# 16-head attention stage: the first head's probability transposes move ahead of the score matmuls in every step

## The reference, cut to what matters

```python
# self (L1_attn): 16 heads of 16 channels, causal
q, k, v = x @ Wq.T, x @ Wk.T, x @ Wv.T                  # split into 16 heads
scores = einsum('...hqd,...hkd->...hqk', q, k) / sqrt(16)
scores = where(causal, -1e9, scores)
out = einsum('...hqk,...hkd->...hqd', softmax(scores), v)
x = layernorm(x + merge_heads(out) @ Wo.T)
# cross (L1_xattn): keys and values from ctx (4, 512, 256), a mask over 512 keys, biases
q, k, v = x @ Wq.T + bq, ctx @ Wk.T + bk, ctx @ Wv.T + bv
scores = where(mask == 0, -1e9, q k / sqrt(16))
x = layernorm(x + merge_heads(softmax(scores) @ v) @ Wo.T + bo)
```

## Time and profile before

| | |
|---|---|
| median of the runs | 4162.72 us |
| the profiled execution: its time, and its span | 4165.06 us, 4163.3 us |
| busy: PE, DVE, ACT, POOL | 93%, 70%, 62%, 30% of the span |
| the 16-head stage, first to last scores | 559.05 to 1210.91 us, 652 us |
| there: PE, DVE, ACT busy | 586.6, 511.9, 455.4 us |
| one body of self attention (the second) | 74.97 us |
| one body of cross attention (the second), the last | 93.91 us, 77.45 us |

### The profile page before, as it was taken

One profiled execution on the slowest core, in us unless ns is written; L12 is line 12 of the kernel. 1 busy time (PEld: TensorE's weight loads), 2 busy tenths in 40 slices (PEclk: granted clock), 3 DMA queues, 4 the chain that ended last, 5 costly groups with the idle time before them and its releaser, 6 DMA issues.

```text
span 4163.3 us, 97842 instructions
## 1 busy us (share of the span) xinstructions
PE 3871.8 (93%) x36632; PEld 2544.0 (61%) x36632; DVE 2904.2 (70%) x10275; ACT 2580.5 (62%) x6856; POOL 1243.2 (30%) x810
## 2 busy tenths in 40 slices
PE   8979578899988999999999999999999999999996
PEld 5668445566655666666666666666666666666664
DVE  3542357788868887777777777777777777777773
ACT  2213246667766767677776676777766766767662
POOL 1103300000005433343434434333434343434330
PEclk9979789999999999999999999999999999999998
DMA  6002210000011001111011101010011101111010
GB/s 181 23 21 73 66 60 2 7 19 22 9 42 29 22 22 48 32 32 27 18 49 30 43 17 53 26 36 24 23 48 32 37 22 38 33 40 29 17 37 18
DMA packets 110785, 146.33 MB, mean 35 GB/s; under 512 B 35748, under 2 KB 77200, under 8 KB 109936
## 3 DMA queue, kind: packets, MB, share of 16 engines
q1 hardware_dynamic: 106912, 130.76, 10.9%
q0 software_dynamic: 3408, 9.31, 0.9%
HBM read 78.31 MB, written 11.40 MB: 22 GB/s over the span
## 4 chain that ended last, share of the span: by engine, by line
PE 54%; DVE 9%; POOL 4%; issue 2%; DMA 1%; ACT 0%; SPq 0%; DVEq 0%; POOLq 0%
PE psum L489 17%; PE psum L586 9%; PE psum L469 7%; PE psum L570 6%; PE psum L603 5%; PE psum L549 4%; PE psum L523 4%; POOL f_rn L892 3%; DVE f_rot L710 2%; DVE f_prob L753 1%; DVE f_rot L712 1%; DVE f_ss L717 1%; DVE f_xn L807 1%; PE psum L592 1%; DVE f_prob L781 1%
## 5 line engine op out<-in xcount | busy, mean ns | idle before, releaser
L489 PE MATMUL psum<-f_wqkv,f_xsT 128*128 128x512 f32 x2304 | 1072.1, 595 | 4.3 <-ACT f_raw L636 2.6
L887 POOL TENSOR_TENSOR f_raw<-f_rot 128x512 f32<-128x512 f32 x384 | 488.7, 1273 | 1663.8 <-DVE f_rot L712 1663.8
L650 ACT ACTIVATE f_prob<-f_prob,f_nb,f_rq 128x128 f32<-128x128 f32 x1536 | 740.1, 487 | 38.6 <-DVE f_nb L766 37.7
L489 PEld LDWEIGHTS psum<-f_wqkv,f_xsT 128*128 128x128 f32 x2304 | 402.5, 191 | 334.2 <-issue 329.4
L892 POOL TENSOR_TENSOR f_rn<-f_ss,f_half_pow 128x32 f32<-128x32 f32 x96 | 524.4, 5463 | 11.2
L586 PE MATMUL psum<-f_xnT,f_w 128*128 128x512 f32 x960 | 437.9, 595 | 2.2 <-ACT f_hT L673 1.1
L753 DVE CUSTOM_DVE_ANT_0 f_prob<-psum,f_band 128x128 f32<-128x128 f32 x1536 | 352.8, 285 | 115.9 <-PE psum L523 114.7
L634 ACT ACTIVATE f_sq<-psum 128x512 f32<-128x512 f32 x384 | 227.8, 593 | 231.1 <-PE psum L489 231.0
L781 DVE TENSOR_SCALAR f_prob<-f_prob,f_rs 128x128 f32<-128x128 f32 x1536 | 341.2, 286 | 13.6
L570 PE MATMUL psum<-f_wo,f_oT 128*128 128x256 f32 x1536 | 347.4, 379 | 1.6 <-ACT f_v L636 0.9
L710 DVE TENSOR_TENSOR f_rot<-f_raw,f_tab 128x512 f32<-128x512 f32 x384 | 333.4, 868 | 14.3 <-DMA x_before_mlp<-x_all 14.3
(11 more groups left out here) (248 smaller groups left out, 6978.3 us busy)
## 6 DMA issues: line engine op xcount, KB each, us to landing
f_v_near<-f_v SPq DMA_DIRECT2D x168, 256.0 KB, 3.5
f_wqkv<-in_Wqkv SPq DMA_DIRECT2D x36, 512.0 KB, 5.8
w_moe_W<-in_L_ffn_W SPq DMA_DIRECT2D x2, 4096.0 KB, 22.4
f_w<-in_W SPq DMA_DIRECT2D x12, 640.0 KB
f_wo<-in_Wo SPq DMA_DIRECT2D x6, 1024.0 KB, 6.4
f_xs<-x_all SPq DMA_DIRECT2D x24, 254.0 KB
expert_rows<-m_y SPq DMA_DIRECT2D x39, 128.0 KB, 1.7
h_mask_int<-in_mask_BxSxS_ik SPq DMA_DIRECT2D x16, 256.0 KB, 2.6
```

Of the source, the lines that this page charges most:

```text
L489: mm = nc.tensor.matmul(ps.ap(step), xsT[:, c, t * P:(t + 1) * P], wqkv[:, c, i * HALF:(i + 1) * HALF], start=c == 0, stop=c == KC - 1)
L650: ex = nc.scalar.activation(pr, pr, ACT.Exp, bias=nb[:, t % 2, h:h + 1], scale=rq8[:, t, h:h + 1], accum_out=sums[:, t % 2, h:h + 1])
L887: nc.gpsimd.tensor_tensor(raw[:, (4 * t + i) % 8, :], rot[:, n % 2, 0, :], rot[:, n % 2, 1, :], ALU.add).then_inc(rope_done, 1)
```

## The change

In every step the first head's transposes (`pt` 0) are written ahead of the scores (`s`), where they stood behind `s`, `max` 0 and `max` 1:

```diff
-                yield ("s", 0, n)
+                yield from [("pt", of(m), m, 0), ("s", 0, n)]
                 if n % 4 == 1:
                     t = (n - 5) // 4
                     yield ("rs", of(t), t % TB)
-                yield from [("max", 0, n, 0), ("max", 0, n, 1), ("pt", of(m), m, 0), ("e", of(e), e, 0),
+                yield from [("max", 0, n, 0), ("max", 0, n, 1), ("e", of(e), e, 0),
                             ("e", of(e), e, 1), ("pt", of(m), m, 1), *first, ("max", 0, n, 2), ("max", 0, n, 3),
                             ("pt", of(m), m, 2), ("e", of(e), e, 2), ("e", of(e), e, 3), ("pt", of(m), m, 3), *second]
```

## The result

The changed kernel takes 4170.67 us (median of 11 runs, 4165.47 to 4180.41), the kernel before 4163.18 us beside it (11 runs). The ratio is 1.0023, 95% interval 1.0016 to 1.0031: slower by about 0.2%, where 4160 and a small gain had been forecast. The time lies in the forecast range of 4150 to 4172, but on the other side of zero. Run once more beside 27 runs of the kernel before, the same code gave 1.0018 (1.0009 to 1.0027).

A forecast was written before the change was run, and what follows sets the result against it. PE was taken as fullest but not full, the engines waiting for each other in a ring. Cross bodies +0.3, last body +3.8 and self bodies -7.5 summed to -3.4 us, giving 4160, range 4150 to 4172.

The forecast's parts named there:

- the tie of `pt` 3 to the scores: Cross step 13: scores, max 0, max 1, DVE's copy of head 1, then `pt` 3 at 3.33, not shortened by the change.
- The moved head costs 0.50 between `pv` and `s`, and saves 0.465 where it stood: PE's price for head 0's transposes at 512 keys: 0.465, plus 0.03 to 0.04 for scores straight behind them.
- The bound of 0.16 extra: Scores straight behind transposes on PE: at most 0.16 extra, the tail of the last transpose, if all of it is waited for.
- the sign that I had named: The forecast would be wrong if `pv` to `s` over head 0 took much more than 1.51.
- output and empty steps: Steps with `wo` or nothing between: `pt` 3 stays at 3.33, so the step grows by 0.5.
- denominator steps: Cross steps 3, 11, 15: head 0 reaches ACT earlier, so each step gains 0.5; step 11 from 5.91 to 5.4.
- query steps: Cross steps full on PE at 5.70 before and after: change 0.
- key steps: Cross steps 2, 10, 14: the projection moves from 2.00 to 1.53, so each gains 0.3; step 10 from 6.03 to 5.73.
- The rival of the change of mode: Scores behind transposes cost more: from 0.03 more, slower than before; at the 0.16 bound +13, 4172 us; chance 0.10.
- More gain: Rival: the ring loosens everywhere and the +0.5 steps cost nothing, 16 us, giving 4144, half of it 4152; chance 0.20.
- The ACT chain: Rival: ACT is not free when head 0 comes, denominator gains of 12.7 us are lost, giving 4172; chance 0.06.
- It does nothing: Rival: DVE sets the ring, both orders give the same and time stays at 4163; chance 0.10.

The follow-up runs named there:

- copy_between: The changed kernel with DVE's copy of head 1 moved ahead of max 1; 4139.18 us, ratio 0.9938 to the kernel before.

## Why the prediction was wrong

*Which engine is waited for, and the tie of `pt` 3 to the scores*: right. The copy, `pt` 3 and `pv` stand where the forecast put them, and copy_between moved all three by moving the copy.

*The moved head costs 0.50 between `pv` and `s`, and saves 0.465 where it stood*: this is the step that failed. It costs 0.58 to 0.59 and saves 0.43, so moving it is priced at 0.15, not at 0.035. I halved a pair (0.93) that stands behind tiled scores, and read 0.04 for the change to tiled matmuls from a pair in front of `pv` (0.97). Both pairs stand next to a tiled group, so their difference nearly cancels what such a place costs. A row with one head in front of `pv` was there: 1026.04 to 1026.60, 0.56. I used that row for the chain and not for the price. The bound of 0.16 extra held (0.12 over 0.465), and the sign that I had named came: `pv` to `s` takes 1.59 (1027.26 to 1028.85), not 1.51.

What it did: output and empty steps +0.6 instead of +0.5, denominator steps -0.42 instead of -0.5; query steps +0.15 instead of 0 (5.70 to 5.85), key steps -0.18 instead of -0.3 (5.85), where the 0.03 less saved comes on top. Setting query steps at 0 also left out the 0.035 of my own prices. Over a cross body that is +1.47 instead of +0.1, three times 1.4; in the last body 1.5; in the second to fourth self bodies, read in the same way, 1.0, 1.0 and 1.5. Together some 9 us of the 12.4 between the forecast -3.4 and the measured +9.05. Some 0.5 of it, in steps 7 and 11 of the fourth self body, has no counterpart in the other self bodies, and its cause stays open. The rival of the change of mode said that from 0.03 more than assumed the kernel is slower; it was 0.08 to 0.09 more. It had 0.10 and should have had most.

*The first self body*: forecast -1.5, measured +2.03. 2.8 of the 3.5 between them are the clock, which I did not consider. Of that up to 1.0 is there in the kernel before in some executions.

*More gain*: fell, for the reason given against it. *The ACT chain*: fell, ACT's copy started at 0.11 instead of 1.77. *It does nothing*: fell, steps changed by up to 0.6 both ways.

*The sum of small terms*: cross body +0.1 was the difference of +2.5 and -2.4, and the whole -3.4 that of about +17 and -20. With 100 places, an error of 0.03 in one price decides the sign, as I wrote; then a chance of 0.14 for slower was too little. That the time still lies in the range is owed to the rivals' 4172, which set its upper end, and not to the forecast.

## What to carry to other kernels

Moving a part forward in an in-order queue pays where another engine sits on its result (here ACT in the denominator steps: 0.5% by that quarter alone). Elsewhere it costs the difference between its old place and its new one (0.15 in query steps), up to its whole length where its old place lay in a wait (0.58 in empty steps). So make the move per place and not in all of them. Look for the second tie before judging a move: an early head 0 in every step gained nothing while the copy of head 1 stood behind two reductions, the earlier copy gained nothing while head 1 was late, and both together gave 0.6%. Where a forecast is a small difference of two large sums, its weight lies in the least known price, and the nearest row has to match it in its count of instructions and in its neighbours as well as in kind: half of a pair is not the price of one.

## What the runs showed of the hardware

- Four transposes of 128x128 in float32 cost 0.43 us when added beside others of their kind. Alone they cost 0.46 after a wait in front of an untiled projection, 0.50 behind the row-tiled scores in front of one, 0.56 after a wait in front of either tiled group, and 0.58 to 0.59 between column-tiled `pv` and row-tiled scores. One semaphore wait on the scores instead of four left that at 0.59.
- The granted clock fell to half at the start of the 16-head stage in the kernel before too, for 3.4 us in one of two profiles, and its first self body took 1.0 us more with it (67.67 against 66.69). 6.8 us at half clock cost 2.8 us in step 4 of the changed kernel.
